# Two graph layers on one core: the value products of four query tiles go from four bursts a round to two, over sixteen turned tiles

## What is computed

```python
B, N, D = x.shape                       # 16, 512, 128;  H = 4 heads, hd = 32
xp = jnp.einsum('mn,bnf->bmf', L_norm, x)
h = relu(_layernorm(xp @ Wc + bc, g1, be1))
x1 = h + x
q, k, v = (split_heads(x1 @ W) for W in (Wq, Wk, Wv))
scores = jnp.einsum('bhnd,bhmd->bhnm', q, k) / sqrt(hd)      # masked where adjacency is 0
attn = jax.nn.softmax(scores, axis=-1)
o = jnp.einsum('bhnm,bhmd->bhnd', attn, v)            # the value products
x2 = _layernorm(x1 + (o @ Wo + bo), g2, be2)
out = _layernorm(x2 + gelu(x2 @ W1 + b1) @ W2 + b2, g3, be3)
```

## Time and profile before

| | |
|---|---|
| median of 3 runs | 882.45 us (881.64 to 884.24) |
| the profiled execution's own time | 881.41 us |
| its span | 879.6 us |
| PE matmul busy | 829.4 us, 94% |
| PE weight load busy | 699.2 us, 79% |
| DVE busy | 649.4 us, 74% |
| ACT busy | 534.0 us, 61% |
| POOL busy | 318.7 us, 36% |

### The profile page before, as it was taken

One profiled execution on the slowest core, in us unless ns is written; L12 is line 12 of the kernel. 1 busy time (PEld: TensorE's weight loads), 2 busy tenths in 40 slices (PEclk: granted clock), 3 DMA queues, 4 the chain that ended last, 5 costly groups with the idle time before them and its releaser, 6 DMA issues.

```text
span 879.6 us, 18960 instructions
## 1 busy us (share of the span) xinstructions
PE 829.4 (94%) x6695; PEld 699.2 (79%) x6695; DVE 649.4 (74%) x2123; ACT 534.0 (61%) x1228; POOL 318.7 (36%) x421
## 2 busy tenths in 40 slices
PE   6999999999999999997999999999999999989993
PEld 5679989898989888985677777777777777768982
DVE  6966464645454746536888999999999998977998
ACT  3244343434343323224988888988888889787884
POOL 2011121212122314400445455555554555423655
PEclk9999999999999999999999999999999999999997
DMA  6000010101010100141555554444556545441253
GB/s 132 0 13 13 13 37 13 37 13 37 13 37 13 37 25 25 60 109 39 130 121 145 145 145 124 116 111 105 126 145 145 145 115 129 113 80 49 74 144 96
DMA packets 51881, 69.64 MB, mean 79 GB/s; under 512 B 4294, under 2 KB 23116, under 8 KB 51788
## 3 DMA queue, kind: packets, MB, share of 16 engines
q1 hardware_dynamic: 51488, 68.31, 30.2%
q10 hardware_dynamic: 300, 0.13, 0.1%
HBM read 43.78 MB, written 24.64 MB: 78 GB/s over the span
## 4 chain that ended last, share of the span: by engine, by line
PE 20%; DVE 17%; issue 7%; DMA 6%; ACT 3%; SPq 1%; DVEq 0%; ACTq 0%
PE bank L1839 6%; DMA q_stack<-bounce_k 4%; PE bank L1859 4%; PE bank L1901 3%; PE bank L1826 3%; DVE prob L2008 3%; DVE stats L1619 2%; DVE probT L1995 2%; DVE z_std L313 2%; DMA bounce_q<-k_parts 2%; SPq L423 1%; ACT prob L1951 1%; PE bank L366 1%; DVE prob L1614 1%; DVE probT L1631 1%
## 5 line engine op out<-in xcount | busy, mean ns | idle before, releaser
L1951 ACT ACTIVATE prob<-prob,low 128x512 f32<-128x512 f32 x256 | 184.3, 720 | 31.4 <-DVE low L2008 29.3
L2008 DVE CUSTOM_DVE_ANT_0 prob<-bank,mask 128x512 f32<-128x512 f32 x256 | 171.0, 681 | 12.0 <-PE bank L1826 9.6
L1839 PE MATMUL bank<-ident,prob 128*128 128x128 f32 x1024 | 157.2, 276 | 1.6 <-ACT probT L1934 1.3
L1839 PEld LDWEIGHTS bank<-ident,prob 128*128 128x128 f32 x1024 | 119.9, 140 | 41.3 <-issue 29.5
L1826 PE MATMUL bank<-k_stack,q_stack 128*128 128x512 f32 x256 | 123.5, 483 | 11.8 <-DVE low L2008 6.3
L1934 ACT ACTIVATE probT<-bank 128x512 f32<-128x512 f32 x176 | 103.8, 590 | 21.0 <-PE bank L1839 20.9
L853 PE MATMUL bank<-B_hi,halves 128*128 128x384 f32 x384 | 105.7, 338 | 1.1 <-DVE halves L1229 1.1
L824 PE MATMUL bank<-halves,P3T_hi 128*128 128x256 f32 x512 | 93.8, 285 | 0.9 <-DVE halves L1258 0.5
L824 PEld LDWEIGHTS bank<-halves,P3T_hi 128*128 128x128 f32 x512 | 80.7, 192 | 4.6 <-DVE halves L1258 1.3
L630 POOL TENSOR_SCALAR var_eps<-mv 128x4 f32<-128x4 f32 x16 | 3.6, 228 | 195.0 <-DVE mv L1179 195.0
L853 PEld LDWEIGHTS bank<-B_hi,halves 128*128 128x128 f32 x384 | 70.1, 188 | 3.7 <-DVE halves L1229 2.1
(11 more groups left out here) (270 smaller groups left out, 1916.5 us busy)
## 6 DMA issues: line engine op xcount, KB each, us to landing
k_stack<-bounce_q SPq DMA_DIRECT2D x64, 256.0 KB, 4.5
q_stack<-bounce_k SPq DMA_DIRECT2D x64, 256.0 KB, 7.6
bounce_q<-k_parts SPq DMA_DIRECT2D x16, 512.0 KB, 3.0
bounce_k<-q_parts SPq DMA_DIRECT2D x16, 512.0 KB, 3.0
x_in<-in_x_dram SPq DMA_DIRECT2D x16, 256.0 KB, 2.9
out_dram<-probT SPq DMA_DIRECT2D x16, 256.0 KB, 2.2
y_shifted<-y_staging SPq DMA_DIRECT2D x14, 256.0 KB, 2.0
probT<-y_shifted SPq DMA_DIRECT2D x14, 256.0 KB, 2.9
```

The lines of the kernel that those rows point to most:

```text
L1839: last = pe.transpose(psum[2 + u % 2][:, mt * P:(mt + 1) * P], prob[u % RING][:, mt * P:(mt + 1) * P], ident[:, :])
L1951: act.activation(prob[u % RING][:, :], prob[u % RING][:, :], ACT.Exp, bias=low[:, u % TURNED:u % TURNED + 1], scale=-1.0, accum_out=row_su ...
L2008: dve.tensor_tensor_reduce(prob[u % RING][:, :], psum[u % 2][:, :], mask[:, u // HEADS, :], 1.0, 3e38, ALU.add, ALU.min, low[:, u % TURNED ...
```

## The change

`x2` becomes a second name of `y`: POOL writes the normalised sum of graph `e` over that graph's part of `y`. The memory that this frees goes to 16 `probT` buffers in place of 8. With them the four tiles can wait longer for their products, and the bursts are put together: tiles 0 and 1 of the attending graph in unit 13, tiles 2 and 3 of the leaving graph in unit 5. DVE's first mask of round 1 gets a wait for `y_written`.

```diff
-VALUES_LAG = 9
-VALUES_STEP = 4
+VALUES_AT = {13: (0, 1), 5: (2, 3)}
...
-TURNED = 8
+TURNED = 16
...
-    x2 = tensor(whole, "x2", [P, BATCH * N])
+    x2 = y
...
-                def values(batch, s, t, first):
-
-                    if first == 0:
+                def values(batch, s, tiles):
+
+                    for t in tiles:
                         tile_units = range(HEADS * t, HEADS * (t + 1))
...
-                    for mt in range(first, first + VALUES_STEP):
-                        for head in range(HEADS):
-                            rows = slice(head * HD, (head + 1) * HD)
-                            last = pe.matmul(psum[6 + s][rows, t * P:(t + 1) * P], v[s][:, mt, rows],
-                                             probT[(HEADS * t + head) % TURNED][:, mt, :],
-                                             start=mt == 0, stop=mt == NT - 1, skip_group_check=True)
-                    if first + VALUES_STEP == NT:
+                    for t in tiles:
+                        for mt in range(NT):
+                            for head in range(HEADS):
+                                rows = slice(head * HD, (head + 1) * HD)
+                                last = pe.matmul(psum[6 + s][rows, t * P:(t + 1) * P], v[s][:, mt, rows],
+                                                 probT[HEADS * t + head][:, mt, :],
+                                                 start=mt == 0, stop=mt == NT - 1, skip_group_check=True)
                         last.then_inc(o_psum, 1)
...
-                        if u % VALUES_STEP == VALUES_LAG % VALUES_STEP:
-                            if u < VALUES_LAG and leaves:
-                                values(e, s, *divmod(u + UNITS - VALUES_LAG, HEADS))
-                            if u >= VALUES_LAG and attends:
-                                values(a, 1 - s, *divmod(u - VALUES_LAG, HEADS))
+                        if u in VALUES_AT:
+                            if 0 not in VALUES_AT[u] and leaves:
+                                values(e, s, VALUES_AT[u])
+                            if 0 in VALUES_AT[u] and attends:
+                                values(a, 1 - s, VALUES_AT[u])
...
+                            if (r, u) == (1, 0):
+                                dve.wait_ge(one.y_written, 16 * STAGED)
```

## The result

| | before | after |
|---|---|---|
| median, timed together | 883.35 us | 895.16 us (894.05 to 897.38) |
| ratio | | 1.0138, interval 1.0115 to 1.0161 |
| profiled execution, its span | 881.41, 879.6 us | 895.74, 893.9 us |
| k of round 2 to k of round 15, 13 rounds | 326.45 us, 25.11 each | 337.26 us, 25.94 each |

The kernel is slower by 12.2 us by the ratio (0.0138 x 883.35; the medians differ by 11.8), clear of noise and inside the range of 890 to 902; the forecast was 16.1 more. In the rows of the kernel after, PE's transposes of turned tiles stand at L1838 (before L1839), its scores at L1825 (L1826), ACT's lines one lower, and DVE's mask one higher, at L2009 (L2008).

What follows compares the result with a forecast made beforehand. Bound: the 25.08 us loop from k to k, through PE's units 3 to 14, DVE, POOL and ACT. 13 x 1.17 = 15.2, + 0.4 + 0.5 = 16.1 us; 882.45 + 16.1 = 898.5 us, range 890 to 902.

Steps and rivals of the forecast that it cites:

- Unit 1 is slack, units 3 to 14 are not: PE time ahead of k is covered by waits, so unit 1's lost burst gains 0; PE holds the loop in units 3 to 14.
- Price of a burst: On PE, a burst of one tile costs 1.17 us; 32 products take 2.02, bounds 2.02 and 2.02 + 0.16.
- Units 5 and 9: Second tile in unit 5 makes turns 1.01 us later; with unit 9's burst gone, both together cost -0.09 us.
- ACT's chain in unit 10: Turn of unit 6 to convolution weights takes 2.56 us: new PE wait of about 0.5 us, unit 10 0.38 late.
- A': Rival: only PE's own work counts, ACT's chain keeps up; round grows by 0.70 us, 892.5 us in all; chance 0.25.
- Unit 13 and DVE's copy of unit 11: Second tile makes turn 11 late by 1.39 us, DVE's copy, after spare 0.22, by 1.17, carried on through `z_std` and POOL.
- Round 1, rounds 15 to 17: Outside the 13 rounds: round 1 costs 0.4 us (0 to 0.8), round 15 0, rounds 16 and 17 0.5 (0 to 1.5).
- y_written, memory, tiles: DVE's wait for the last write of y (over 28 us of cover), x2 in y's memory and 16 turned tiles: cost 0.
- Signs: Rounds 26.2 us; 64-record bursts; convT wait in unit 10; DVE's largest wait at copy 11; PE waits about 2 us, units 0-3.
- Fewer switches (B): Rival: PE's total sets the time; two bursts fewer save 0.32 us a round, 4.8 in 15 rounds: 877.6 us; chance 0.07.
- C: Rival, no change: double bursts absorbed between the turn of unit 11 and `z_std`; 881 to 885 us; chance 0.05.
- D: Rival, worse: late turns also delay exponentials or mask 15; 1.6 us a round and more, 903 us or over; chance 0.08.

Runs made afterwards that it cites:

- e1: Changed kernel with its bursts back in the old units (tile 0 in 9, 1 in 13, 2 in 1, 3 in 5): 883.5 us, 1.0004 to before.
- e3: Changed kernel with only tiles 2 and 3 together, in unit 5; tile 0 in unit 9, tile 1 in 13: 895.1 us, 1.0151 to before.
- e5: Changed kernel with four single bursts in the old units, except tile 1 in unit 15, not 13: 888.4 us, 1.0065 to before.
- e2: Changed kernel with only tiles 0 and 1 together, in unit 13; tile 2 in unit 1, tile 3 in 5: 885.8 us, 1.0032 to before.
- e4: Changed kernel with both double bursts taken apart: tile 0 in unit 12, 1 in 13, 2 in 4, 3 in 5: 902.1 us, 1.0218 to before.
- e6: Changed kernel with four single bursts: tile 0 in unit 13, 1 in 15, 2 in 1, 3 in 5: 882.0 us, 0.9987 to before.
- e8: Changed kernel with tiles 0 and 1 together in unit 15, tile 2 in unit 1, tile 3 in 5: 895.2 us, 1.0138 to before.

## Why the prediction was right, and what it had wrong

- *Unit 1 is slack, units 3 to 14 are not.* Right, and it is the cause. The old places give the old time (e1), and e3 shows that moving tile 2 from unit 1 into unit 5 costs the 12 us by itself. Of units 3 to 14 it is true only up to the turn of unit 7 in the kernel before: a burst in unit 13 was beside the path (e3, and e5, whose round stays 25.08 without it).
- *Price of a burst.* The step that was mis-sized: I took 2.02 us for 32 products and it was 1.89. A second tile costs 0.88, not 1.01. Twice 0.13 is 0.26 a round, 3.4 of the 4.4 us by which the rounds' term missed. The lower bound of 2.02 was no bound: twice the time of a burst of its own also counts twice whatever such a burst has at its start or end beyond its products. Which of the two holds the 0.13 no run shows.
- *Units 5 and 9.* Forecast: the turn of unit 7 comes 0.09 us sooner behind k. Measured: 628.54 - 617.91 = 10.63 against 10.91, 0.28 sooner.
- *ACT's chain in unit 10.* Right in kind: turn of unit 6 to the convolution's weights took 2.48 us (forecast 2.56), a wait in each of 13 rounds. Unit 10 was 0.10 late (11.74 behind k against 11.64), not 0.38. PE, started again after the wait, also needs 0.99 for the step over the weights (629.65 to 630.64), 0.10 more than without a wait. Without wait and restart the turn of unit 11 would have been -0.28 + 0.88 = 0.60 late and not 1.07, so ACT's chain is nearly half of the growth. A' falls in kind, though the time, 895.2, lies in the middle between A' (892.5) and the forecast (898.5): the number alone would not have told them apart, and the two misses, a burst too dear and a chain too long, lie on the same side.
- *Unit 13 and DVE's copy of unit 11.* Turn 11 stood 17.61 behind k against 16.54, +1.07 (forecast +1.39), less the spare 0.22: 0.85 for 1.17. The 0.22 was right here, since the path now does lead over PE to that turn; as a reading of before it was wrong, as e3 showed (0.82 for 0.66).
- *13 rounds.* 15.2 forecast, 10.8 measured.
- *Round 1, rounds 15 to 17.* k of round 1 to k of round 2: 0.47 more (0.4 forecast). The granted clock was 0.94 there and 1.00 before, so this match proves little alone; e2, with the same burst in unit 13 and 1.00, has 0.37 more. Behind scores 0 of round 16: 101.68 us against 100.49, 1.2 more (0.5, bound 1.5). The stack of round 15 landed 0.8 us later behind k (18.67 against 17.87), which I had set at 0.
- *y_written, memory, tiles.* Cost 0, by e1, within its interval. SP issued the last write at 377.65, DVE's first mask stood at 406.37.
- *Signs.* Came: bursts of 64 records, PE's wait for convT in each round, DVE's wait gone ahead of the copy of unit 7. Rounds were 25.94 and not 26.2. Didn't come: DVE's largest wait is not the one ahead of the copy of unit 11 (0.57 us, for 0.8 to 0.9), since the masks behind the double burst of unit 5 wait more. PE's waits in units 0 to 3 are 0.18 + 0.78 + 0.27 = 1.23 us in rows and not 2; most of the rest stands in two longer steps, ahead of the turn of unit 15 and of the scores behind it.
- *Rivals.* Fewer switches (B) named a real saving, 0.29 for two bursts merged by e4, more than the 0.16 that I read around a burst; it needs the place. The Trainium skill says in TensorEngine Tiling (Array Packing), section Tiling Modes, that changing the tiling mode drains TensorE. The trace agrees in that a merged burst costs less than two; how much of the 0.29 us is a drain no run shows. C and D didn't come.

## What to carry to other kernels

Follow the loop that brings an instruction back to itself, with the number of each link, before moving work on the busiest engine: PE, busy for 97% of a round, had a stretch in which a burst of 1.17 us cost nothing, and another in which a second tile of 0.88 cost 0.82. Merge bursts where it saves, but put the merged burst beside the loop, and check both the queue of its own engine and the slower loops behind it (here the way of q and k through DRAM, for which PE waited up to 0.83 us a round in e6, once the other loop was shorter). When a wait vanishes at one place, ask whether the waiter came later or the awaited sooner: DVE's 0.82 us ahead of the copy of unit 7 vanished because DVE's masks were late.

## What was not expected of the hardware

The granted clock fell in short stretches that differ from run to run. The stages view of the kernel after (columns as in the earlier trace rows), early in the first layer and at the change of layers, and two rows of PE's timeline from there:

```profile
60.00:62.00 2.00, 2.00 (x8) 2.00 (x7) 0.00 (x0) 1.78 (x5) 0.91 (x1) 0.50 0.00 0
...
406.00:408.00 2.00, 1.15 (x4) 0.37 (x2) 1.63 (x5) 0.89 (x3) 0.96 (x1) 0.99 0.00 0
408.00:410.00 2.00, 2.00 (x10) 1.66 (x9) 0.90 (x3) 2.00 (x3) 0.00 (x0) 0.50 0.00 0
```

```profile
405.68 0.71 PE L1825 MATMUL bank<-k_stack,q_stack 128*128 128x512 f32 x2 [1.05 <-PEq L572]
...
409.25 1.06 PE L1838 MATMUL bank<-ident,prob 128*128 128x128 f32 x4
```

0.50 is the lower level, 1.2 GHz, and the four transposes take 1.06 us in place of 0.60. The profile of before has 1.00 from 60 to 70 and from 405 to 415 us. From 400 us to k of round 1 all profiles but that of before have a mean of 0.82 to 0.88; the timed runs of before have mean clocks from 0.985 to 0.993 over the whole, so that the dips are not a mark of the change. Ahead of the second dip PE waited 1.05 us at the change of layers, and again for DVE. Two of the four timed runs of the kernel after had a mean granted clock of 0.986 (895.74 and 897.38 us), two 0.992 (894.05 and 894.58); the 13 rounds ran at 1.00. Of the 1.5 us between the profiles ahead of k of round 2, 1.0 stood already at k of round 1, which e1 to e8 put anywhere from 409.6 to 413.2 us.
